# Two engines for the cross products: GpSimd takes three of five chunks in units without gathers

## The chip, the cores and the metric

The kernel runs on one core of a Trainium2 chip. The metric is the device time of one execution, in microseconds (us), lower is better. The core has five engines that run unsynchronised and hand work on by semaphores: TensorE (PE in the profile), VectorE (DVE), ScalarE (ACT), GpSimd (POOL) and SyncE (SP), whose queue issues most of the DMAs.

## The reference

A recommender tower over a batch of 1024 rows, in f32. For each row 50 embeddings of 300 numbers are gathered, two attention heads pool them, and a layer makes h (300 numbers). The heavy part is the product of all pairs of h with a matrix of 44,850 rows:

```python
q1 = _attn_pool(x, mask, w1, b1, w2)
q2 = _attn_pool(x, mask, w3, b3, w4)
h = jnp.concatenate([q1, q2], axis=1) @ w5 + b5
f6 = h @ w6 + b6
iu, ju = jnp.triu_indices(E, k=1)
g = (v @ v.T)[iu, ju]
cross = h[:, iu] * h[:, ju] * g
f7 = cross @ w7 + b7
out8 = jnp.concatenate([f6, f7], axis=1) @ w8 + b8
return jnp.einsum('bu,bku->bk', out8, label_embedding)
```

The last line takes 200 dot products of each row with its own label embeddings (246 MB read once). Three small layers (the top) follow on these 200 results and 16 context numbers.

## The kernel before

The batch is cut into 8 tiles of 128 rows. The cross products of a tile come in 71 units, and two tiles are in work at a time, staggered, so there are 325 units (u = 0 to 324). Units 41 to 283 hold two tiles, units 0 to 40 the first tile alone, and units 284 to 324 the last (tile 7) alone. A unit is a block of five chunks (three in a folded unit). For each unit:

- SP loads `w7` rows of the unit into one of four places of `w_sb` (line 670), which needs the unit four before it used.
- PE turns a block of h into the PSUM tile `coarse` (line 1014), one such window for two units. The other factor lies in SBUF as `fine`, refilled for each part of a round.
- DVE multiplies `fine` by `coarse` into `prod`, all five chunks in one instruction (`cross`, line 930). `prod` has three places, so cross(u) needs unit u-3 used.
- ACT scales each chunk by g (line 1474), in order, and between chunks copies windows, sums absolute values of gathered rows (line 1369) and answers PE's bursts.
- PE multiplies each chunk by its `w7` rows into `acc` (line 1223). The trace has two records for each such product, so a unit of two tiles is 20 records and of one tile 10.

Between the crosses DVE does, in an order fixed by `plan()`, the other work: `dots` (scores of a tile's embeddings, line 772), `wsums` (the weighted sums, line 820, in ten halves a tile), and `slab` (the label dot products, line 772, 8 label rows each; 25 slabs a tile, numbered 0 to 199 through the batch). A slab of a tile needs the tile's out8, which comes after its 71st unit. Nine slabs of tile 7 are multiplied by GpSimd (line 746) and summed by ACT (line 1379). The slabs are loaded by SP too (line 692), in one queue with the `w7` loads, in the order of the table `LOADS`. A slab's load waits for its place to be free: 4 places, later 10, and 3 more for the end.

GpSimd issues the gathers of the embeddings, one instruction a field (line 711), 50 a tile, in groups of five, each group behind the weighted sums of the tile before it that free its rows. When a tile's slabs are all done, its top (four bursts on PE: line 1072, 1078, 1085, 1123) runs where `schedule()` finds room.

`plan()` walks through time with a table of costs (0.1 us each) and writes down which item DVE takes behind which cross, and the order of the loads.

Of the kernel before, what the change touches and what calls it, by code (L numbers as in the profile page):

```python
# [13 lines left out]
P = 128  # L14
# [8 lines left out]
FINE = 5  # L23
# [39 lines left out]
DIAGS = 10  # L63
JUNK = 3
LAB_FIELDS = SLOTS * SLAB
# [140 lines left out]

def plan():

# [23 lines left out]
    while c < TOTAL or len(slab_end) < len(slabs):  # L232
        u, nslab, due, held = c - 1, len(slab_end), 1e9, False
        if c < TOTAL:
            due = FIRST_CROSS if c < 2 else begun[c - 2] + 0.45 * UNIT[len(active(c - 2))]
            held = bool(rest) and c > STARTS[rest[0][1]] - 8
            if now >= due and not held:
                now = max(now, ended[c - RING]) + CROSS[len(active(c))]
                begun[c] = max(ended[c - 1], now + 15)
                ended[c] = begun[c] + UNIT[len(active(c))]  # L240
                if c + W7_RING < TOTAL:
                    loads.append((ended[c], "w7", c + W7_RING))
                c += 1
                continue
# [75 lines left out]


BEFORE, ITEMS, TAIL, POOL_TICKS, LOADS, SWITCH = plan()
LABELLED = {item[1]: u for u in range(TOTAL) for item in ITEMS[u] if item[::2] == ("slab", SLABS - 1)}

# [107 lines left out]
def order_last_loads(loads):  # L432


    extra = [("slab", LAST + END_SLOTS + n) for n in range(EXTRA_SLOTS)]
    loads = [load for load in loads if load not in extra]
    loads.insert(loads.index(("w7", TOTAL - 1)) + 1, extra[0])
    loads.insert(loads.index(("slab", LAST + END_SLOTS - 2)), extra[1])
    loads.insert(loads.index(("slab", LAST + END_SLOTS - 1)) + 1, extra[2])
    return loads  # L440
# [10 lines left out]
def dlrm_tower(nc, ids, tables, labels, ctx_in, w_score, b_rep, w5, w6, b7_in, w7, w8a_in, w8b,  # L451
               v_i, v_j, top1, bias1, top2, bias2, top3, ident_in, y_out):
    with ExitStack() as ctx:
# [18 lines left out]
        top3_sb = sb("top3_sb", [P, M2])  # L472
        pads = sb("pads", [P, FIELDS])
        g_all = sb("g_all", [P, CHUNKS])
# [17 lines left out]
        dup = sb("dup", [P, 2, 2, P])  # L492
        picked = sb("picked", [P, PICKED, 2, P])
        prod = sb("prod", [P, RING, FINE, 2 * P])
        w7_sb = sb("w7_sb", [P, W7_RING, FINE * EMB])
# [3 lines left out]
        big = sb("big", [P, 2 * ECN * P])  # L499
        small = sb("small", [P, EMB])  # L500
        qt = big[:, 0:QCN * P]
# [3 lines left out]
        h1t = big[:, 0:M1 * P]  # L505
        f7s = small[:, 0:EMB]
        zt = small[0:ZC, 0:ZCN * P]
# [63 lines left out]
        fine_ready = sem("fine_ready")  # L571
        chunk_ready = sem("chunk_ready")
        unit_used = sem("unit_used")
        pe_step = sem("pe_step")
# [69 lines left out]
        def _(sp):  # L644
# [20 lines left out]
            for kind, n in LOADS:  # L665
# [14 lines left out]
                elif n == LAST + END_SLOTS:  # L680
                    sp.wait_ge(cross_ready, FREE_FINE)
                elif n == LAST + END_SLOTS + 1:
                    sp.wait_ge(unit_used, PAIR_USED)
# [13 lines left out]
        def _(pool):  # L697
# [51 lines left out]
        def _(dve):  # L749
            dve.memset(ones, 1.0).then_inc(filled, 1)  # L750
            dve.memset(pads[:], PAD).then_inc(filled, 1)
            for r in range(JUNK):
# [36 lines left out]
            def mask(t):  # L789
# [5 lines left out]
                for head in range(2):  # L795
                    dve.copy_predicated(score[:, t % 2, head, :], empty[:], pads[:]).then_inc(chain, 1)
                then(t, 4)
# [190 lines left out]
        def _(pe):  # L988
# [14 lines left out]
            def turn_coarse(u):  # L1003
# [6 lines left out]
                if w >= 2:  # L1010
                    pe.wait_ge(cross_ready, last_unit(w - 2) + 1)
                rows = rows_of(u)
                for t in active(u):
# [225 lines left out]
        def _(act):  # L1239
# [10 lines left out]
            def pick_window(u):  # L1250
# [215 lines left out]
            for u in range(TOTAL):  # L1466
                rows = rows_of(u)
                slot, n = slots_of(u)
                act.wait_ge(cross_ready, u + 1)
                for m in range(FINE):  # L1470
                    if m < chunks_of(u):
                        chunk = prod[0:rows, u % RING, m, slot * P:(slot + n) * P]
                        pair = u % UNITS * FINE + m
# [7 lines left out]
                    for name, t, i in POOL_TICKS.get(tick, ()):  # L1481
# [4 lines left out]
                        elif name == "exp_softmax":  # L1486
                            exp_softmax(t)
            respond("f7s", TILES - 1, 0, 0)
            for name, of, n in END_BURSTS:
                for summed in {"zt": range(2), "z_first": range(2, FIRST_SUMS),  # L1490
                               "z_rest": range(FIRST_SUMS, len(BY_POOL))}.get(name, ()):
                    sum_rows(summed)
                respond(name, of, n, TILES % 3)
# [91 lines left out]
```

## Time and profile before

| | |
|---|---|
| median of 3 runs | 1827.76 us (1826.76 to 1828.46) |
| the profiled execution | 1827.58 us |
| its span, first to last instruction | 1825.8 us |
| PE busy, share of the span | 1686.1 us, 92% |
| DVE busy | 1658.0 us, 91% |
| ACT busy | 1014.6 us, 56% |
| POOL busy | 576.0 us, 32% |
| mean granted clock of TensorE | 0.975 |
| moved by DMA | 561.69 MB, mean 308 GB/s |

Busy time is the time in which an engine had an instruction in work. Matmuls overlap and their ends are modelled. The 1.8 us around the span are not in the trace.

### The profile page before, as it was taken

The numbers are of one execution on the slowest core, as the hardware profiler recorded it, in microseconds if no ns is written. First come the engines' busy times: TensorE is split into PE (matmuls) and PEld (weight loads), VectorE is DVE, ScalarE is ACT, GpSimd is POOL, SyncE is SP. The second block draws the span as 40 slices with busy tenths as digits, with TensorE's granted clock in tenths as the row PEclk, the third lists the DMA queues.
The fourth block names the chain that finished last, engine by engine and source line by source line (L and its number), as shares of the span: only waits on it lengthen the run. The fifth ranks groups of instructions, "written<-read, shape, count | busy, mean of one in ns | idle before, by whom it ended". The sixth has DMA issues, their size and how long they took to land.

```text
span 1825.8 us, 25763 instructions
## 1 busy us (share of the span) xinstructions
PE 1686.1 (92%) x6990; PEld 1243.0 (68%) x6990; DVE 1658.0 (91%) x5831; ACT 1014.6 (56%) x3183; POOL 576.0 (32%) x420
## 2 busy tenths in 40 slices
PE   2888999999999999999999999999999999997755
PEld 1645667777767777777777777767776677775545
DVE  5988989989999889999999999899999888957678
ACT  3776693684357644456554674445754344354536
POOL 7777806828300044500067108700000000000027
PEclk8899999999999999999999999999999999999986
DMA  9488856857987689888878866998648999989996
GB/s 276 108 274 297 308 179 209 326 169 278 381 329 296 244 318 373 328 363 322 299 243 307 318 248 204 352 418 352 229 161 341 420 420 377 417 306 419 418 415 264
DMA packets 98221, 561.69 MB, mean 308 GB/s; under 512 B 16799, under 2 KB 17157, under 8 KB 72477
## 3 DMA queue, kind: packets, MB, share of 16 engines
q1 hardware_dynamic: 77917, 498.35, 70.8%
q0 software_dynamic: 19424, 61.65, 10.7%
q8 instruction: 57, 0.93, 0.2%
q14 instruction: 87, 0.71, 0.1%
q10 hardware_dynamic: 736, 0.05, 0.0%
HBM read 559.98 MB, written 0.00 MB: 307 GB/s over the span
## 4 chain that ended last, share of the span: by engine, by line
PE 44%; DVE 33%; DMA 9%; POOL 6%; issue 6%; ACT 2%; SPq 0%; DVEq 0%; POOLq 0%; ACTq 0%
PE acc L1223 38%; DVE junk L772 12%; DVE qa L820 12%; DVE prod L930 8%; DMA w_sb<-in_w 8%; POOL x L711 4%; POOL lab L711 2%; DMA lab<-in_labels 1%; ACT waste L1369 1%; PE coarse L1014 1%; PE acc L1061 1%; PE acc L1064 1%; PE misc L1026 1%; PE coarse L1118 1%; PE acc L1046 1%
## 5 line engine op out<-in xcount | busy, mean ns | idle before, releaser
L1223 PE MATMUL acc<-w_sb,prod 128*128 128x300 f32 (+2 forms) x5648 | 1510.7, 421 | 62.9 <-DMA w_sb<-in_w 35.0
L1223 PEld LDWEIGHTS acc<-w_sb,prod 128*128 128x128 f32 (+2 forms) x5648 | 1048.2, 191 | 430.4 <-issue 52.7
L1474 ACT ACTIVATE prod<-prod,g_all 128x256 f32<-128x256 f32 (+4 forms) x1615 | 675.0, 470 | 477.1 <-DVE prod L930 472.4
L711 POOL DMA_INDIRECT x<-in_tbl,ids_sb x368 | 488.4, 1327 | 644.5 <-DVE qa L820 534.2
L930 DVE TENSOR_TENSOR prod<-fine,coarse 128x1280 f32<-128x1280 f32 (+3 forms) x320 | 418.6, 1314 | 85.1 <-PE coarse L1014 69.3
L772 DVE SCALAR_TENSOR_TENSOR junk<-lab,heads 128x300 bf16<-128x300 f32 x1192 | 471.1, 459 | 12.6 <-DMA lab<-in_labels 7.7
L772 DVE SCALAR_TENSOR_TENSOR junk<-x,heads 128x300 bf16<-128x300 f32 x1112 | 439.0, 460 | 24.0 <-DMA x<-in_tbl,ids_sb 23.6
L820 DVE SCALAR_TENSOR_TENSOR qa<-x,ex,qa 128x300 f32<-128x300 f32 x612 | 275.4, 520 | 0.1
L746 POOL TENSOR_TENSOR x<-x,out 128x2400 f32<-128x2400 f32 x4 | 21.2, 5288 | 583.3 <-ACT out L1326 583.3
L1369 ACT ACTIVATE waste<-x 128x300 bf16<-128x300 f32 x368 | 161.6, 439 | 26.0 <-DMA x<-in_tbl,ids_sb 25.2
L1294 ACT ACTIVATE fine<-misc 128x512 f32<-128x512 f32 (+3 forms) x67 | 36.3, 542 | 112.3 <-PE misc L1026 83.7
L772 DVE DVE_READ_ACCUMULATOR junk<-lab,heads 128x1 f32 x1192 | 96.1, 81 | 0.0
L772 DVE DVE_READ_ACCUMULATOR junk<-x,heads 128x1 f32 x1112 | 90.0, 81 | 0.0
L1369 ACT ACTIVATION_READ_ACCUMULATOR waste<-x 128x1 f32 x368 | 69.3, 188 | 0.0
L1271 ACT ACTIVATE picked<-hh 128x256 f32<-128x256 f32 (+5 forms) x165 | 61.3, 372 | 0.0
L1014 PE MATMUL coarse<-ident,picked 128*128 128x128 f32 (+2 forms) x288 | 58.9, 274 | 0.0
L1014 PEld LDWEIGHTS coarse<-ident,picked 128*128 128x128 f32 (+2 forms) x288 | 40.7, 141 | 24.4 <-issue 0.4
L1198 PE MATMUL acc<-x,fine 128*128 128x300 f32 x88 | 24.6, 443 | 22.0 <-ACT fine L1417 22.0
L711 POOL DMA_INDIRECT lab<-in_tbl,ids_sb x32 | 35.9, 1123 | 9.8 <-issue 9.8
L1198 PEld LDWEIGHTS acc<-x,fine 128*128 128x128 f32 x88 | 17.6, 203 | 29.1 <-issue 21.5
L1078 PE MATMUL acc<-small,top_sb 108*128 108x128 f32 x112 | 15.5, 297 | 14.1 <-ACT small L1248 14.1
L820 DVE SCALAR_TENSOR_TENSOR qa<-lab,ex,qa 128x300 f32<-128x300 f32 x60 | 27.1, 520 | 0.0
(142 smaller groups left out, 604.2 us busy)
## 6 DMA issues: line engine op xcount, KB each, us to landing
w_sb<-in_w SPq DMA_DIRECT2D x320, 750.0 KB, 6.8
lab<-in_labels SPq DMA_DIRECT2D x144, 1200.0 KB, 8.7
x<-in_labels SPq DMA_DIRECT2D x51, 1200.0 KB, 12.0
x<-in_tbl,ids_sb POOLq DMA_INDIRECT x368, 5.5
fine<-in_labels SPq DMA_DIRECT2D x2, 1200.0 KB, 11.1
prod<-in_labels SPq DMA_DIRECT2D x2, 1200.0 KB, 13.6
w_sb<-in_w SPq DMA_DIRECT2D x5, 450.0 KB, 4.5
w_sb<-in_labels SPq DMA_DIRECT2D x1, 1200.0 KB, 12.4
```

The costliest lines, as they stand in the source:

```text
L711: pool.indirect_dma_start(out=row_of(t, n), out_offset=None, in_=tables[n], in_offset=bass.IndirectOffsetOnAxis(ap=ids_sb[:, t % IDS_RING, ...
L746: pool.tensor_tensor(slab_place(slot), slab_place(slot), row8, ALU.mult).then_inc(multiplied, 1)
L772: dve.scalar_tensor_tensor(unused, in0, 1.0, in1, ALU.mult, ALU.mult, accum_out=out).then_inc(rows_done, 1)
L820: dve.scalar_tensor_tensor(part, row_of(t, n), ex[:, head, n:n + 1], part, ALU.mult, ALU.add).then_inc(wsum_done, 1)
L930: dve.tensor_tensor(prod[0:rows, u % RING, 0:chunks, slot * P:(slot + n) * P], sets[0:rows, made:made + chunks, slot * P:(slot + n) * P], ...
L1014: last = pe.transpose(coarse[0:rows, w % 2, t % 2 * P:(t % 2 + 1) * P], picked[:, w % PICKED, t % 2, 0:rows], ident[:])
L1198: pe.matmul(sums[:, head, 0:EMB], diag[:, k % DIAGS, :], x[:, n, :], start=i < 2, stop=i >= PE0[group] - 2).then_inc(diag_used, 1)
L1223: last = pe.matmul(acc[:, t % 3, 0:EMB], prod[0:rows, u % RING, m, t % 2 * P:(t % 2 + 1) * P], w7_sb[0:rows, u % W7_RING, m * EMB:(m + 1) ...
L1271: act.activation(out, cols, ACT.Copy).then_inc(picked_ready, 1)
L1294: act.activation(sets[0:rows, at + ms[0]:at + ms[-1] + 1, slot * P:(slot + tiles) * P], made[:, :, slot * P:(slot + tiles) * P], ACT.Copy) ...
L1369: act.activation(waste[:, n % 2, :], row_of(t, n), ACT.Abs, accum_out=absum[:, t % 2, n:n + 1]).then_inc(abs_done, 1)
L1474: act.activation(chunk, chunk, ACT.Copy, scale=g_all[0:rows, pair:pair + 1]).then_inc(chunk_ready, 1)
```

## The change

In the units in which GpSimd has no gathers to issue (`SHARED`, 177 of 325), DVE's cross makes only the first two chunks. ACT copies the window from PSUM to a new SBUF tile `kept` (91 copies), and GpSimd makes the other three from it (`share_of`). ACT waits for them ahead of the third chunk. The shared units are 37 to 49, 62 to 72, 92 to 108, 132 to 150, 173 to 186, 207 to 234 and 248 to 324, without the folded ones. 133 have two tiles and 44 have one. GpSimd's shares of such a stretch stand in its queue behind the last gather of one tile and ahead of the first gather of the next.

The planner counts 0.7 us for a cross of two tiles where it counted 1.4, so the order of DVE's items and of the loads changes. To make room, `junk` has two places and not three, `pads` is one column read with step 0, and `f7s` moves from `small` to `dup`.

```diff
-JUNK = 3
+JUNK = 2
+SHARE = 3
+POOL_CROSS = (0, 4, 7)
-def plan():
+def plan(pooled):
...
-                now = max(now, ended[c - RING]) + CROSS[len(active(c))]
+                now = max(now, ended[c - RING]) + (POOL_CROSS if c in pooled else CROSS)[len(active(c))]
...
-BEFORE, ITEMS, TAIL, POOL_TICKS, LOADS, SWITCH = plan()
+GATHERS_END = 4
+def free_of_gathers(items):
+    busy = [[u for u in range(TOTAL) for kind, of, _ in items[u] if (kind, of) == ("wsums", t)]
+            for t in range(1, TILES)]
+    until = [units[0] + 1 for units in busy[1:]] + [TOTAL]
+    return [[u for u in range(units[-1] + GATHERS_END, end) if not folded(u)]
+            for units, end in zip(busy, until)]
+PLAN = plan(())
+for _ in range(2):
+    PLAN = plan(frozenset(u for units in free_of_gathers(PLAN[1]) for u in units))
+BEFORE, ITEMS, TAIL, POOL_TICKS, LOADS, SWITCH = PLAN
+AFTER_GATHERS = free_of_gathers(ITEMS)
+SHARED = frozenset(u for units in AFTER_GATHERS for u in units)
+def own_chunks(u):
+    return chunks_of(u) - SHARE * (u in SHARED)
...
@@ GpSimd @@
+            def share_of(u):
+                slot, n = slots_of(u)
+                cols = slice(slot * P, (slot + n) * P)
+                rows, made = rows_of(u), first_set(u) + (not opens(u)) * FINE
+                pool.wait_ge(window_kept, windows_kept(u))
+                pool.wait_ge(fine_ready, fills_before(u))
+                pool.wait_ge(unit_used, u - RING + 1)
+                window = kept[0:rows, cols]
+                window = bass.AP(tensor=window.tensor, offset=window.offset,
+                                 ap=[list(window.ap[0]), [0, SHARE], [1, n * P]])
+                pool.tensor_tensor(prod[0:rows, u % RING, own_chunks(u):FINE, cols],
+                                   fine_sets[0:rows, made + own_chunks(u):made + FINE, cols],
+                                   window, ALU.mult).then_inc(shared_ready, 1)
             for t in range(2, TILES):
...
                     gather(t, n)
...
+                for u in AFTER_GATHERS[t - 2]:
+                    share_of(u)
+            for u in AFTER_GATHERS[TILES - 2]:
+                share_of(u)
@@ VectorE, cross(u) @@
+                if not opens(u) and keeps_window(u - 1):
+                    dve.wait_ge(window_kept, windows_kept(u))
...
-                rows, chunks = rows_of(u), chunks_of(u)
+                rows, chunks = rows_of(u), own_chunks(u)
@@ ScalarE @@
+            def keep_window(u):
+                w = window_of(u)
+                slot, n = slots_of(u)
+                rows, cols = rows_of(u), slice(slot * P, (slot + n) * P)
+                act.wait_ge(coarse_ready, w + 1)
+                act.activation(kept[0:rows, cols], coarse[0:rows, w % 2, cols], ACT.Copy
+                               ).then_inc(window_kept, 1)
...
                 act.wait_ge(cross_ready, u + 1)
+                if keeps_window(u):
+                    keep_window(u)
                 for m in range(FINE):
                     if m < chunks_of(u):
+                        if m == own_chunks(u):
+                            act.wait_ge(shared_ready, shares_up_to(u))
```

The first place is GpSimd's queue, from the gathers of tile 2 on. Before, gathers follow on gathers:

```order
L711 DMA x<-in_tbl,ids_sb 128x300 x18
L705 DMA ids_sb<-in_ids 128x50
L711 DMA x<-in_tbl,ids_sb 128x300 x26
L705 DMA ids_sb<-in_ids 128x50
L711 DMA x<-in_tbl,ids_sb 128x300 x50
L705 DMA ids_sb<-in_ids 128x50
```

Of the change, from the same place:

```order
L760 DMA ids_sb<-in_ids 128x50
L766 DMA x<-in_tbl,ids_sb 128x300 x24
L795 ISA
L795 TENSOR_TENSOR prod<-fine,kept 126x3x128 x4
L795 TENSOR_TENSOR prod<-fine,kept 128x768 x9
L766 DMA x<-in_tbl,ids_sb 128x300 x26
L760 DMA ids_sb<-in_ids 128x50
L766 DMA x<-in_tbl,ids_sb 128x300 x24
L795 TENSOR_TENSOR prod<-fine,kept 128x768 x11
```

The shares of units 37 to 49 (4 of one tile, 9 of two) stand behind the last gather of tile 2, and the shares of units 62 to 72 (x11) behind all 50 gathers of tile 3, which are the 26 and 24 rows ahead of them. An `ISA` row stands ahead of the first product; before it stood ahead of line 746's.

The second place is the end of SP's queue, in the last units. `w_sb<-in_w` is a unit's `w7`, the others are slabs. Before, from the load of unit 318's `w7` on:

```order
L670 DMA w_sb<-in_w 128x1500 x2
L692 DMA lab<-in_labels 128x2400
L670 DMA w_sb<-in_w 128x1500 x2
L692 DMA lab<-in_labels 128x2400
L670 DMA w_sb<-in_w 128x1500
L692 DMA fine<-in_labels 128x2400
L692 DMA x<-in_labels 128x2400
```

Of the change, from the load of unit 316's `w7` on:

```order
L724 DMA w_sb<-in_w 128x1500 x2
L747 DMA lab<-in_labels 128x2400
L724 DMA w_sb<-in_w 128x1500
L747 DMA lab<-in_labels 128x2400
L724 DMA w_sb<-in_w 128x1500
L747 DMA lab<-in_labels 128x2400
L724 DMA w_sb<-in_w 128x1500
L747 DMA x<-in_labels 128x2400
L724 DMA w_sb<-in_w 128x1500 x4
L747 DMA fine<-in_labels 128x2400
```

From slab 160, which stands behind unit 290's `w7` in both, to unit 324's `w7` there are 22 slab loads before and 25 in the change; to unit 320's `w7`, 20 and 24. Slabs 182 to 184 stand behind the last `w7` before, and ahead of it in the change. Over the whole queue the slab loads ahead of unit 240's `w7` go from 109 to 122.

The tops move as well: tile 5's from units 286 to 288 to units 274 to 276, tile 6's from behind the last unit to units 319 to 321.

## Rows read from the trace of the kernel before

**Rows 1.** Busy time (and count) of PE, PEld, DVE, ACT, POOL; granted clock, DMA share, GB/s.

```profile
190.00:1400.00 1210.00, 1191.34 (x5024) 888.89 (x5023) 1166.50 (x3869) 691.05 (x2061) 382.88 (x277) 1.00 0.78 291
1400.00:1640.00 240.00, 233.73 (x996) 175.69 (x995) 196.19 (x754) 107.71 (x285) 0.00 (x0) 0.99 0.97 390
1640.00:1760.00 120.00, 95.40 (x356) 65.03 (x355) 90.26 (x371) 57.57 (x205) 0.00 (x0) 0.96 1.01 419
```

**Rows 2.** PE's waits from 190 to 1640, then to 235: total, times, longest.

```profile
PE acc L1223 <- ACT prod L1474: 13.4, 24, 1.8
PE acc L1223 <- DMA w_sb<-in_w: 10.7, 6, 3.0
...
PE acc L1223 <- ACT prod L1474: 3.6, 7, 1.4
```

**Rows 3.** The tail: GpSimd's first product, two of DVE's rows.

```profile
1767.47 5.25 POOL L746 TENSOR_TENSOR x<-x,out 128x2400 f32<-128x2400 f32 x1 [583.31 <-ACT out L1326]
...
1772.56 0.46 DVE L772 SCALAR_TENSOR_TENSOR junk<-x,heads 128x300 bf16<-128x300 f32 x1
1772.95 0.46 DVE L772 SCALAR_TENSOR_TENSOR junk<-x,heads 128x300 bf16<-128x300 f32 x1
```

**Rows 4.** Groups by form: cross of two tiles, of one, ACT's chunk, GpSimd's product.

```profile
L930 DVE TENSOR_TENSOR prod<-fine,coarse 128x1280 f32<-128x1280 f32 x210 | 310.4, 1480 | 35.9 <-PE coarse L1014 34.1 <-PE acc L1223 1.6 <-issue 0.2
L930 DVE TENSOR_TENSOR prod<-fine,coarse 128x640 f32<-128x640 f32 x60 | 47.9, 815 | 34.9 <-PE coarse L1014 24.0 <-PE acc L1223 10.9
L1474 ACT ACTIVATE prod<-prod,g_all 128x256 f32<-128x256 f32 x1050 | 468.8, 497 | 357.5 <-DVE prod L930 353.3 <-ACT z L1248 2.9 <-issue 1.0
L746 POOL TENSOR_TENSOR x<-x,out 128x2400 f32<-128x2400 f32 x4 | 21.2, 5288 | 583.3 <-ACT out L1326 583.3
```

**Rows 5.** PE's waits at 1412 and 1423, and the clock around them.

```profile
1412.76 4.99 PE L1223 MATMUL acc<-w_sb,prod 126*128 126x300 f32 x12 [2.16 <-DMA w_sb<-in_w]
1423.23 1.47 PE L1223 MATMUL acc<-w_sb,prod 126*128 126x300 f32 x4 [3.02 <-DMA w_sb<-in_w]
...
1410.00:1430.00 20.00, 14.81 (x51) 10.19 (x50) 17.31 (x71) 5.55 (x15) 0.00 (x0) 0.83 1.01 422
```

**Rows 6.** PE in time from unit 61 on: start, us, records.

```profile
349.96 0.38 PE L1014 MATMUL coarse<-ident,picked 128*128 128x128 f32 x2
350.18 10.49 PE L1223 MATMUL acc<-w_sb,prod 128*128 128x300 f32 x40
```

**Rows 7.** GpSimd's gathers of tile 3, 283 to 376 us: the group, then two single ones.

```profile
L711 POOL DMA_INDIRECT x<-in_tbl,ids_sb x50 | 76.3, 1526 | 69.4 <-DVE qa L820 54.8 <-issue 14.6
...
332.00 4.25 POOL L711 DMA_INDIRECT x<-in_tbl,ids_sb  x1 [0.30 <-issue]
...
374.74 0.95 POOL L711 DMA_INDIRECT x<-in_tbl,ids_sb  x1 [0.30 <-issue]
```

**Rows 8.** Tile 4's last gather, and DVE's cross of unit 92.

```profile
505.77 0.95 POOL L711 DMA_INDIRECT x<-in_tbl,ids_sb  x1 [0.30 <-issue]
...
518.59 1.48 DVE L930 TENSOR_TENSOR prod<-fine,coarse 128x1280 f32<-128x1280 f32 x1
```

**Rows 9.** The last gather of tile 2, and PE in unit 37.

```profile
228.43 0.95 POOL L711 DMA_INDIRECT x<-in_tbl,ids_sb  x1 [0.30 <-issue]
...
230.18 1.18 PE L1223 MATMUL acc<-w_sb,prod 126*128 126x300 f32 x4
```

**Rows 10.** SP issues slab 160; PE starts units 320 and 324.

```profile
1626.08 0.33 SPq L692 DMA_DIRECT2D lab<-in_labels  x1
...
1745.16 3.30 PE L1223 MATMUL acc<-w_sb,prod 126*128 126x300 f32 x12 [1.57 <-DMA w_sb<-in_w]
...
1758.33 2.79 PE L1223 MATMUL acc<-w_sb,prod 126*128 126x300 f32 x10 [1.21 <-DMA w_sb<-in_w]
```

**Rows 11.** A slab's load in the page's DMA issues: KB each, us to landing.

```profile
lab<-in_labels SPq DMA_DIRECT2D x144, 1200.0 KB, 8.7
```

**Rows 12.** A burst of tile 5's top on PE.

```profile
1624.17 1.95 PE L1078 MATMUL acc<-small,top_sb 108*128 108x128 f32 x16
```

More of the change, by code:

```diff
@@ L319, in plan, with shares_up_to, keeps_window, windows_kept @@
     return before, items, tail, pool_ticks, loads, switch
-BEFORE, ITEMS, TAIL, POOL_TICKS, LOADS, SWITCH = plan()
+GATHERS_END = 4
[13 more added lines that the diff above has]
+    return chunks_of(u) - SHARE * (u in SHARED)
+def shares_up_to(u):
+    return sum(v in SHARED for v in range(u + 1))
+def keeps_window(u):
+    return u in SHARED and not (u - 1 in SHARED and window_of(u - 1) == window_of(u))
+def windows_kept(u):
+    return sum(keeps_window(v) for v in range(u + 1))
+def windows_kept_up_to(w):
+    return sum(keeps_window(v) for v in range(TOTAL) if window_of(v) <= w)
 LABELLED = {item[1]: u for u in range(TOTAL) for item in ITEMS[u] if item[::2] == ("slab", SLABS - 1)}
@@ L437, in order_last_loads @@
     loads.insert(loads.index(("w7", TOTAL - 1)) + 1, extra[0])
-    loads.insert(loads.index(("slab", LAST + END_SLOTS - 2)), extra[1])
-    loads.insert(loads.index(("slab", LAST + END_SLOTS - 1)) + 1, extra[2])
+    weights_end = loads.index(extra[0]) + 1
+    loads.insert(max(weights_end, loads.index(("slab", LAST + END_SLOTS - 2))), extra[1])
+    loads.insert(max(weights_end + 1, loads.index(("slab", LAST + END_SLOTS - 1)) + 1), extra[2])
     return loads
@@ L472, in dlrm_tower @@
         top3_sb = sb("top3_sb", [P, M2])
-        pads = sb("pads", [P, FIELDS])
+        pad = sb("pad", [P, 1])
+        pads = bass.AP(tensor=pad[:].tensor, offset=pad[:].offset,
+                       ap=[list(pad[:].ap[0]), [0, FIELDS]])
         g_all = sb("g_all", [P, CHUNKS])
@@ L493, in dlrm_tower @@
         picked = sb("picked", [P, PICKED, 2, P])
+        kept = sb("kept", [P, 2 * P])
         prod = sb("prod", [P, RING, FINE, 2 * P])
@@ L499, in dlrm_tower @@
         big = sb("big", [P, 2 * ECN * P])
-        small = sb("small", [P, EMB])
+        small = sb("small", [P, 2 * P])
         qt = big[:, 0:QCN * P]
@@ L505, in dlrm_tower @@
         h1t = big[:, 0:M1 * P]
-        f7s = small[:, 0:EMB]
+        f7s = dup[:].rearrange("p m t b -> p (m t b)")[:, 0:EMB]
         zt = small[0:ZC, 0:ZCN * P]
@@ L572, in dlrm_tower @@
         chunk_ready = sem("chunk_ready")
+        window_kept = sem("window_kept")
+        shared_ready = sem("shared_ready")
         unit_used = sem("unit_used")
@@ L681, in _ @@
                     sp.wait_ge(cross_ready, FREE_FINE)
+                    sp.wait_ge(shared_ready, shares_up_to(FREE_FINE - 1))
                 elif n == LAST + END_SLOTS + 1:
@@ L750, in _ @@
             dve.memset(ones, 1.0).then_inc(filled, 1)
-            dve.memset(pads[:], PAD).then_inc(filled, 1)
+            dve.memset(pad[:], PAD).then_inc(filled, 1)
             for r in range(JUNK):
@@ L795, in mask @@
                 for head in range(2):
-                    dve.copy_predicated(score[:, t % 2, head, :], empty[:], pads[:]).then_inc(chain, 1)
+                    dve.copy_predicated(score[:, t % 2, head, :], empty[:], pads).then_inc(chain, 1)
                 then(t, 4)
@@ L1011, in turn_coarse @@
                     pe.wait_ge(cross_ready, last_unit(w - 2) + 1)
+                    if windows_kept_up_to(w - 2):
+                        pe.wait_ge(window_kept, windows_kept_up_to(w - 2))
                 rows = rows_of(u)
@@ L1488, in _ @@
             respond("f7s", TILES - 1, 0, 0)
+            summed = 0
             for name, of, n in END_BURSTS:
-                for summed in {"zt": range(2), "z_first": range(2, FIRST_SUMS),
-                               "z_rest": range(FIRST_SUMS, len(BY_POOL))}.get(name, ()):
-                    sum_rows(summed)
+                for slab in range(summed, {"zt": 2, "z_first": FIRST_SUMS,
+                                           "z_rest": len(BY_POOL)}.get(name, summed)):
+                    sum_rows(slab)
+                    summed = slab + 1
                 respond(name, of, n, TILES % 3)
```

## The prediction

> **What bounds the kernel now.** I read the busy time in stretches first, then PE's waits, then the timelines at the places where the new queue order matters. From 190 to 1400 us both PE (1191 of 1210) and DVE (1167) look full, the clock is 1.00 and DMA is at 0.78 [rows 1]. PE's idle time is the one that can be won back: 19 us there, 6 us from 1400 to 1640, and by releaser 13.4 us for ACT's chunks and 10.7 us for `w7` [rows 2]. So in the two-tile units PE sets the pace and DVE only just keeps up; what DVE gains shows up to about 24 us and no further. From 1640 to 1760 it is another kernel: one tile, PE busy 95 of 120, DMA share 1.01 at 419 GB/s. Each unit waits for its `w7` behind the slabs in the same queue. After the last unit comes a tail in which GpSimd's nine products run end to end [rows 3] with DVE's rows beside them.
>
> **The change, part by part.**
>
> *DVE.* A cross of 1280 elements takes 1480 ns, one of 640 takes 815 [rows 4]: 1.04 ns an element and 0.15 us fixed. Two chunks of two tiles (512) make 0.68, of one (256) 0.42. Saved: 133 x 0.80 + 44 x 0.40 = 124 us of DVE's time. It is worth only what it takes off PE's waits. Of the 13.4 us for chunks, 3.6 lie before 235 us and unit 37 [rows 2], where nothing is shared. Of the 10.7 us for `w7`, 5.2 are the waits at 1412 and 1423 us [rows 5]. They come from the burst of loads when six more places open: up to unit 251's `w7` that burst has eleven slabs in both tables, so they stay. That leaves 9.8 + 5.5 = 15 us. The lateness stems mostly from units with weighted sums, which are not shared, so I take half: **-7 us** (bounds 0 and -15).
>
> *GpSimd's product.* 2400 elements take 5288 ns [rows 4], 2.2 ns each: 768 make 1.69 us, 384 make 0.85, if time goes with length; above, it is bounded by the row itself, 5.29. ACT's cycle for a unit becomes: copy of the window, about 0.45 (as long as a chunk, 0.50), the product, two handoffs of 0.1, and three chunks of at most 0.50: 3.8 us against PE's 5.16 (20 records in 10.49 us by 40, [rows 6]). It stays hidden up to a product of about 3.0 us. I take 1.69, since the nine products of the tail run at 2.2 ns with DVE's rows beside them. DVE's rows there are 0.39 apart for 300 elements [rows 3], so they aren't slowed either.
>
> What DVE does beside GpSimd matters: a gather takes 4.25 us beside the weighted sums, which have both inputs in SBUF, and 0.95 beside the label rows and scores, whose second input is in PSUM [rows 7]. A cross is of the second kind. Only the shares of a stretch's last unit (49, 72, 108, 150, 186, 234) meet weighted sums and may come 4.25 - 0.95 = 3.3 us late. PE is two units (10 us) behind at that point, so it is hidden; I count **+1** (bounds 0 and 6 x 3.3 = 20, the latter without any cover).
>
> The Trainium skill (SBUF — State Buffer, "Who interferes with whom") has this as a rule: a DVE instruction with two SBUF inputs shuts out a GpSimd instruction that reads SBUF for its whole length, one with a single SBUF input doesn't. The trace agrees for the gathers; by the rule too the sum would be 1863, and against shares laid beside all of DVE's work it would speak loudly.
>
> *The shares of units 62 to 72.* This is the largest term. They stand behind all 50 gathers of tile 3, and the change moves none of those: their pace is set by the weighted sums in units 49 to 58, which aren't shared. GpSimd gathers until 374.74 + 0.95 = 375.7 [rows 7]; after the last `qa` beside it, near 336, it issues one each 1.25 us (0.95 and 0.30 of issue) and waits for nobody, so it is simply behind. PE starts unit 62 at 350.18 + 16 records x 0.26 = 354.3 and its third chunk at 356.4 [rows 6]. In the change that chunk is there at 375.7 + 1.69 + 0.2 + ACT's 0.50 = 378.1. ACT waits ahead of it, DVE at cross 65 (its place in `prod` is not free), SP with its `w7` loads: nothing covers it. **+21.7 us.** The idle PE then loses clock: after waits of 2 and 3 us the clock was 0.83 over 20 us [rows 5], 3.4 us; over the 10 us behind one wait **+1.7**. Fifty gathers take 92 us here; the later stretches have their weighted sums over 17 or more units, not ten. There GpSimd keeps up: tile 4's gathers end 12 us ahead of cross 92, where the next stretch of shares begins [rows 8].
>
> *Unit 37.* The last gather of tile 2 ends at 229.4, PE takes the third chunk at 230.2 [rows 9]. With 0.3 + 0.85 + 0.1 + 0.39 it comes at 231.0, and ACT, full with sums of absolute values there, is some 2 us behind afterwards: **+3** (bounds 1 and 7: the first product as long as the row of 2400 elements, 5.3 us for 0.85, adds 4). The Trainium skill (GPSIMD Engine Reference, "Instruction dispatch") gives about 6 us for the first call of a freshly loaded GpSimd routine; if the ISA row is such a load, the term would be 9 and the sum 1869 by it. No row here shows it: before, it fell in idle time.
>
> *The last stage.* Slab 160's load is issued at 1626.08, after tile 6's out8, in both orders; unit 320 starts at 1745.16 when its `w7` lands [rows 10]. A slab is 1200 KB [rows 11], at 419 GB/s 2.93 us. The change puts four more slabs ahead of unit 320's `w7`: +11.7. From there before needed 15.9 us to the end of unit 324 (1761.1); now the four `w7` come in a row and PE is the limit: 5 x 2.58 plus tile 6's top, 4.3 us (1.8 for a burst like that of [rows 12], 1.95 less its overlap, twice, and 0.7 for two small ones) makes 17.2: +1.3. Tile 5's top, 4.3 us, was in the time after slab 160's issue, where PE had to wait for data anyway; now it is in units that PE bounds: +4.3. Against it, PE without that top reaches the DMA's limit sooner after slab 160, so a little of the 119 us comes back; I take -2. Together **+15** (bounds 5 and 18). Nothing is given back in the tail: it has three loads fewer, but its length is nine products of 5.22 us on GpSimd and ACT's sums behind them, started by out8.
>
> *Two places for junk.* A row waits for the one two before it. That ended 0.32 us before this one starts (0.39 apart, 0.46 long [rows 3]), and its accumulator is read at once: nothing. The rest (`pads`, `dup`) moves no work.
>
> **Sum.** 1827.6 (the profiled execution, 0.2 below the median) - 7 + 1 + 21.7 + 1.7 + 3 + 15 = **1863 us**, 1.9% slower.
>
> **The rivals.**
> 1. *The last stage is neutral* (0.14). If the slabs' order there is free, because DVE or the places hold SP up before the bandwidth does, the 15 us fall away: 1848. For it: SP waits for slab places all through. Against: share 1.01 for 120 us.
> 2. *GpSimd is free by unit 62* (0.05). If the five gathers of a group took 7 us, as the planner counts, and not 9.2, the 23.4 us fall away: 1840. Against: the last gather's row [rows 7].
> 3. *DVE paces it* (0.04), the one that ends faster. 97 two-tile units between 41 and 247 save 0.80 each, 77 us. If PE's records hid waits for DVE, these would come out: 1828 - 77 + 42 = 1793. It decides once DVE costs PE more than 42 us there; the trace shows 13.4 [rows 2].
> 4. *GpSimd's product is longer than 3.0 us* (0.06), by a fixed cost or by standing still beside DVE. At 4 us ACT's cycle is about 6.1: 0.9 x 133 on top, about 1980.
> 5. *Rivals 1 and 2 together* (0.03) make 1825, within 0.2% of before.
>
> That the change doesn't free DVE, because DVE waits for `kept` as long as it saves, only takes the 7 us away: 1870, within the forecast's own range.
>
> The forecast itself has 0.68, its own range 1850 to 1878. 0.2% (3.7 us) is what a measurement can tell. Faster 0.04, same 0.03, slower 0.93. The range of 1842 to 1886 takes in rival 1 and the bounds of unit 37, of the shares beside weighted sums and of the 15 us; it leaves out rivals 2 to 5.
>
> **What the profile after would show.** GpSimd goes from its last gather of tile 3 straight to eleven products; PE has one wait of about 20 us for ACT's chunk near 360 us, and DVE one just as long a little later, with a dip of the clock. GpSimd's product of 128x768 takes 1.7 us. PE's `w7` waits at 1410 to 1430 (shifted by some 25 us) are still there; between slab 160's issue and unit 320 lie about 129 us and not 119. The tail from out8 is as long as before. If the wait near 360 us is short, or the last stage isn't longer, the forecast falls with it; a PE wait for ACT in most shared units would be rival 4.

## The result, and the profile after

The changed kernel takes 1875.0 us (median of 4, 1871.3 to 1878.5) against 1827.6 for the kernel before beside it: a ratio of 1.026 [1.024, 1.028]. The forecast was 1863 with a range of 1842 to 1886. Slower was right, and the wait forecast at unit 62 was right to a tenth. The shares earn more than the forecast had, the new table costs more, and a part of the table's cost had no term at all. The profiled execution took 1878.5 us, 50.9 more than before's.

The busy time in stretches answers to [rows 1]; the columns are the same, and the stretches are moved by the time lost ahead of them:

```profile
190.00:1400.00 1210.00, 1165.54 (x4903) 869.14 (x4902) 1107.91 (x3984) 693.40 (x2079) 537.99 (x379) 0.99 0.79 296
1400.00:1680.00 280.00, 266.03 (x1122) 197.53 (x1121) 158.00 (x661) 130.36 (x347) 75.15 (x47) 0.99 0.80 315
1680.00:1811.00 131.00, 102.30 (x384) 68.27 (x383) 72.85 (x347) 61.20 (x219) 29.01 (x30) 0.93 0.99 406
```

DVE was busy 1166 us in the first stretch and is now busy 1108: it has been freed, as planned. PE, which set the pace, is busy 26 us less in the same time, so it stands more. The second line holds what the forecast did not have: the DMA share from 1400 on was 0.97 and is 0.80.

PE's waits from 190 to 1690 answer to [rows 2]:

```profile
PE acc L1302 <- ACT prod L1566: 42.2, 28, 21.6
PE acc L1302 <- DMA w_sb<-in_w: 18.4, 14, 3.1
```

One wait makes half of the first line. The timeline of GpSimd and then of PE, and the clock over 20 us, at units 62 and 63 ([rows 6, 7] are the same place before):

```profile
378.17 0.95 POOL L766 DMA_INDIRECT x<-in_tbl,ids_sb  x1 [0.30 <-issue]
379.15 1.81 POOL L795 TENSOR_TENSOR prod<-fine,kept 128x768 f32<-128x768 f32 x1
...
381.55 6.90 PE L1302 MATMUL acc<-w_sb,prod 128*128 128x300 f32 x16 [21.65 <-ACT prod L1566]
...
373.00:393.00 20.00, 11.45 (x36) 8.34 (x37) 9.04 (x43) 11.65 (x41) 10.13 (x8) 0.65 0.28 85
```

The first product begins directly behind the last gather, and PE's third chunk of unit 62 comes 21.65 us late. The granted clock averaged 0.65 over the 20 us around the end of that wait. Taken in parts it was 0.50 from 381 to 385 us, so PE began again at 1.2 GHz and not at 2.4, and 0.89 in the 8 us behind. The DMA share is down to 0.28 over the 20 us: the places of `w_sb` come free only as PE goes on.

Unit 37, to be set beside [rows 9]:

```profile
229.67 1.96 POOL L795 TENSOR_TENSOR prod<-fine,kept 126x384 f32<-126x384 f32 x2
...
231.17 1.50 PE L1302 MATMUL acc<-w_sb,prod 126*128 126x300 f32 x4 [2.93 <-ACT prod L1566]
```

The groups by form of DVE's two chunks, GpSimd's product for two tiles and for one, ACT's copy of the window, and GpSimd's product of the tail, beside [rows 4]:

```profile
L1007 DVE TENSOR_TENSOR prod<-fine,coarse 128x512 f32<-128x512 f32 x110 | 75.3, 684 | 153.9 <-ACT kept L1361 69.9 <-PE coarse L1093 47.8 <-issue 29.9
L795 POOL TENSOR_TENSOR prod<-fine,kept 128x768 f32<-128x768 f32 x110 | 197.9, 1820 | 424.4 <-ACT kept L1361 418.7 <-PE acc L1302 5.7
L795 POOL TENSOR_TENSOR prod<-fine,kept 128x384 f32<-128x384 f32 x30 | 29.6, 998 | 91.7 <-ACT kept L1361 82.1 <-PE acc L1302 9.4
L1361 ACT ACTIVATE kept<-coarse 128x256 f32<-128x256 f32 x57 | 21.4, 375 | 46.3 <-DVE prod L1007 46.1
L821 POOL TENSOR_TENSOR x<-x,out 128x2400 f32<-128x2400 f32 x4 | 21.0, 5258 | 10.6 <-ACT out L1414 10.6
```

DVE's price, taken from the slope of [rows 4], held: 0.684 us and 0.68 forecast. GpSimd's, taken in proportion to the length, was 1.69 and is 1.82: 768 and 384 elements show a fixed 0.18 us under the 2.1 ns an element. GpSimd is idle ahead of its two-tile products for 418.7 us, waiting for the copy, so it has time to spare once its gathers are done. But two engines now wait that didn't before, ACT for GpSimd's product and DVE for the copy:

```profile
ACT prod L1566 <- POOL prod L795: 75.8, 66, 22.4
DVE prod L1007 <- ACT kept L1361: 117.5, 18, 10.7
```

Of ACT's 75.8 us, 22.4 are unit 62. DVE's 117.5 us are nearly as much as the 124 us that the shares save it. The forecast named this case, in which the change doesn't free DVE. What these waits cost by themselves was not tested; the shares paid with such waits in place (58.6 us of them in the kernel `share_clean` below).

In the last stage SP issues slab 160, PE begins its last 30 records (units 322 to 324), and GpSimd's tail begins ([rows 10] and [rows 3] before):

```profile
1664.07 0.33 SPq L747 DMA_DIRECT2D lab<-in_labels  x1
...
1803.37 7.84 PE L1302 MATMUL acc<-w_sb,prod 126*128 126x300 f32 x30
...
1817.55 10.46 POOL L821 TENSOR_TENSOR x<-x,out 128x2400 f32<-128x2400 f32 x2 [10.61 <-ACT out L1414]
```

PE ends unit 324 at 1811.2, 147.1 us after slab 160's issue, where before needed 135.0. From GpSimd's first product of the tail to the end of the span it is 59.0 us, before 58.3: the tail gave nothing back.

### The profile page after: what moved, and what is told of

Same layout as the page of the kernel before. It is cut to its first block, busy times and chain, and to the rows that moved or that the text cites. A ratio compares the mean times of both kernels' runs of the same rounds, so it can differ in the third digit from the quotient of the medians.

```text
span 1876.6 us, 26315 instructions
## 1 busy us (share of the span) xinstructions
PE 1692.3 (90%) x6990; PEld 1244.2 (66%) x6990; DVE 1545.9 (82%) x5830; ACT 1043.3 (56%) x3274; POOL 834.7 (44%) x597
## 4 chain that ended last, share of the span: by engine, by line
PE 41%; DVE 31%; DMA 10%; POOL 9%; issue 6%; ACT 2%; SPq 0%; ACTq 0%; DVEq 0%; POOLq 0%
PE acc L1302 35%; DVE junk L847 16%; DVE qa L895 8%; DMA w_sb<-in_w 8%; POOL x L766 7%; DVE prod L1007 6%; POOL lab L766 2%; DMA lab<-in_labels 2%; PE misc L1105 1%; PE coarse L1093 1%; ACT waste L1457 1%; PE acc L1125 1%; PE coarse L1197 1%; ACT prod L1566 1%; PE acc L1140 1%
## 5 line engine op out<-in xcount | busy, mean ns | idle before, releaser
L1566 ACT ACTIVATE prod<-prod,g_all 128x256 f32<-128x256 f32 (+4 forms) x1615 | 682.5, 470 | 428.7 <-DVE prod L1007 347.4
L795 POOL TENSOR_TENSOR prod<-fine,kept 128x768 f32<-128x768 f32 (+3 forms) x177 | 283.8, 1622 | 739.1 <-ACT kept L1361 722.1
L766 POOL DMA_INDIRECT x<-in_tbl,ids_sb x368 | 463.8, 1260 | 269.3 <-DVE qa L895 160.5
L1007 DVE TENSOR_TENSOR prod<-fine,coarse 128x512 f32<-128x512 f32 (+7 forms) x320 | 296.2, 930 | 257.4 <-ACT kept L1361 117.5
L847 DVE SCALAR_TENSOR_TENSOR junk<-lab,heads 128x300 bf16<-128x300 f32 x1256 | 496.7, 462 | 6.4 <-DMA lab<-in_labels 3.7
L847 DVE SCALAR_TENSOR_TENSOR junk<-x,heads 128x300 bf16<-128x300 f32 x1048 | 413.3, 462 | 23.4 <-DMA x<-in_tbl,ids_sb 22.9
L847 DVE DVE_READ_ACCUMULATOR junk<-lab,heads 128x1 f32 x1256 | 104.7, 83 | 0.0
L1361 ACT ACTIVATE kept<-coarse 128x256 f32<-128x256 f32 (+3 forms) x91 | 31.8, 349 | 74.0 <-DVE prod L1007 73.8
L1277 PEld LDWEIGHTS acc<-x,fine 128*128 128x128 f32 x88 | 17.8, 206 | 28.4 <-issue 21.1
```

The source lines that it names most:

```text
L766: pool.indirect_dma_start(out=row_of(t, n), out_offset=None, in_=tables[n], in_offset=bass.IndirectOffsetOnAxis(ap=ids_sb[:, t % IDS_RING, ...
L795: pool.tensor_tensor(prod[0:rows, u % RING, own_chunks(u):FINE, cols], fine_sets[0:rows, made + own_chunks(u):made + FINE, cols], window, ...
L847: dve.scalar_tensor_tensor(unused, in0, 1.0, in1, ALU.mult, ALU.mult, accum_out=out).then_inc(rows_done, 1)
L1007: dve.tensor_tensor(prod[0:rows, u % RING, 0:chunks, slot * P:(slot + n) * P], sets[0:rows, made:made + chunks, slot * P:(slot + n) * P], ...
L1277: pe.matmul(sums[:, head, 0:EMB], diag[:, k % DIAGS, :], x[:, n, :], start=i < 2, stop=i >= PE0[group] - 2).then_inc(diag_used, 1)
L1566: act.activation(chunk, chunk, ACT.Copy, scale=g_all[0:rows, pair:pair + 1]).then_inc(chunk_ready, 1)
```

## The experiments

Two parts of the change can be separated. `AFTER_GATHERS` (and `SHARED`, made from it) says which units are shared. The planner's lower price for shared units (`POOL_CROSS`) says where the items between units stand, and with them the label slabs and the order of the loads. I call the table that the planner gives at the old price the old table.

**Where the shares wait for gathers.** `late62` begins the second stretch of shares at unit 67:

```diff
 AFTER_GATHERS = free_of_gathers(ITEMS)
+AFTER_GATHERS[1] = [u for u in AFTER_GATHERS[1] if u >= 67]
```

> The changed kernel, with units 62 to 66 taken out of the shared ones (VectorE makes all five of their chunks), so that the stretch behind tile 3's gathers begins at unit 67; order of items and loads unchanged. Theory T (shares of unit 62 stand behind the last gather, PE waits 21.65 us there and loses a few more to the clock): no such wait, about 25 us less, 1850 us (1845 to 1856). Rival R1 (the shares cost their time everywhere, by the wait for the kept copy and GpSimd's own pace, and unit 62 only shows what would come elsewhere): 1870 us or more. Rival R2 (the delay at unit 62 is given back later, since VectorE then has room): 1872 to 1878 us.

1855.6 us (1853.6 to 1858.3), 19.4 below the changed kernel. The long wait is gone, and R1 and R2 fall. It is 19.4 and not 25 in part because a wait of 3.31 us at unit 65, which the long one had covered, now shows (below). `late62_37` leaves out units 37 to 40 as well:

```diff
+AFTER_GATHERS[0] = [u for u in AFTER_GATHERS[0] if u >= 41]
+AFTER_GATHERS[1] = [u for u in AFTER_GATHERS[1] if u >= 67]
```

> As late62, and units 37 to 40 not shared either (that stretch begins at unit 41). Theory T: the 2.93 + 0.43 us of PE's waits at unit 37 and the clock behind them go as well, 3 to 6 us less than late62: about 1845 us (1840 to 1851). Rival (the 3 us at unit 37 are the first product's own start-up and move to unit 41): equal to late62 within 1 us.

1854.0 us (1852.7 to 1854.3). Less than expected: 1.6 us, and the two kernels' times overlap, so a cost of unit 37 isn't shown clear of the noise. PE has no wait above 0.5 us from unit 37 to 45, so nothing moved there either. But 26.4 us over before are left, with no unit waiting for a gather. (R1 to R9 are the rivals in these expectations; those of the prediction are called by their numbers below.)

**Shares without the new table, and the table without shares.** `share_old_order` takes away the planner's second and third pass:

```diff
 PLAN = plan(())
-for _ in range(2):
-    PLAN = plan(frozenset(u for units in free_of_gathers(PLAN[1]) for u in units))
```

> The shares of the changed kernel with the planner's table of the kernel before: items between the units and order of the loads are those of before (182 slabs ahead of the last w7 block, not 185), 194 units are shared. Theory T: units 62 and 37 still wait (25 + 6 us), the last stage and the label batches fall back to before's (the 15 to 20 us of the later part go): 1858 us (1852 to 1865). Rival R1 (the sharing itself costs in the last stages, by GpSimd's pace or contention): 1873 us or more. Rival R3 (VectorE's freed time pays once the order is old): 1850 us or less.

1865.1 us (1858.6 to 1868.2), a tenth above T's range. With this table two more stretches begin ahead of their tile's last gather. PE's waits at units 37, 62, 177 and 207:

```profile
230.44 3.81 PE L1300 MATMUL acc<-w_sb,prod 126*128 126x300 f32 x7 [2.95 <-ACT prod L1564]
...
380.66 3.87 PE L1300 MATMUL acc<-w_sb,prod 128*128 128x300 f32 x7 [21.71 <-ACT prod L1564]
...
1030.68 2.37 PE L1300 MATMUL acc<-w_sb,prod 126*128 126x300 f32 x4 [9.06 <-ACT prod L1564]
...
1215.21 2.37 PE L1300 MATMUL acc<-w_sb,prod 128*128 128x300 f32 x4 [14.50 <-ACT prod L1564]
```

They make 48.2 us, more than the whole 37.5 that this kernel is over before. So something pays. `order_alone` is the other half, the new table with DVE doing all five chunks:

```diff
-AFTER_GATHERS = free_of_gathers(ITEMS)
+AFTER_GATHERS = [[] for _ in range(1, TILES)]
```

> The changed kernel's order of items and loads, but no unit is shared: VectorE makes all five chunks everywhere, as before. Theory T: no waits at units 62 and 37; the order costs 15 to 20 us in the last stages as in the changed kernel, and some more where items stand between units for which VectorE has no time now: 1852 us (1843 to 1870). Rival R1 (the sharing costs, the order is free): 1828 to 1833 us.

1890.8 us (1890.0 to 1891.8): 63 over before, far beyond both theories' numbers. The direction was T's, the size was not. PE's waits from 190 to 1690 account for 39 of the 63 (62.7 us, where [rows 2] has 24.1 up to 1640); ACT's chunks are late 50 times and not 24:

```profile
PE acc L1302 <- ACT prod L1566: 50.1, 50, 3.3
PE acc L1302 <- DMA w_sb<-in_w: 12.6, 9, 3.2
```

The table has work placed for a DVE that is quicker in the shared units, and without shares DVE has not the time. It means too that on this table the shares are worth 15.8 us even with their wait at unit 62, and 36.8 without it (`late62_37`).

**The shares alone.** `share_clean` is `share_old_order` with each stretch beginning where the last gather is over:

```diff
 AFTER_GATHERS = free_of_gathers(ITEMS)
+AFTER_GATHERS = [[u for u in units if u >= first]
+                 for units, first in zip(AFTER_GATHERS, (41, 70, 92, 140, 182, 212, 248))]
```

> The shares of the changed kernel with the planner's table of before (as share_old_order), and each shared stretch begins only where the tile's last gather is over in that run's trace (units 41, 70, 92, 140, 182, 212 and 248 on): 168 units are shared. Theory T (what costs is units that stand behind gathers, and the new order; the sharing itself neither costs nor pays, since PE's own work and, at the end, the loads of w7 set the pace): 1829 us (1824 to 1835). Rival R1 (GpSimd's pace, the kept copy or contention cost in every shared unit): 1840 us or more. Rival R3 (VectorE's freed time pays once nothing waits for gathers): 1820 us or less.

1815.5 us (1813.6 to 1816.8), a ratio to before of 0.993 [0.991, 0.995]: a small gain, but clear of the noise, and 59.5 us under the changed kernel. My theory (1829) missed by 13 us; R3 came out. The four waits for gathers, 48.2 us, account for nearly all of the 49.6 us between `share_old_order` and this kernel. `old_order_alone` is the control, with the changed kernel's other edits, the old table and no share:

```diff
+AFTER_GATHERS = [[] for _ in range(1, TILES)]
```

> The changed kernel's code with the planner's table of before and no shared unit: only its other edits are left (two junk buffers, the constant of one column, the f7s copy in the dup buffer, the smaller scratch, the end's bookkeeping). Theory T (the 12 us that share_clean gained on before come from the sharing, by fewer of PE's waits for chunks in units 90 to 250): 1827.5 us within 2. Rival R6 (they come from the other edits): about 1815 us.

1827.9 us, ratio 1.0007 [0.9997, 1.0016]. The gain is the shares'. `clean_to248` drops the last stretch of shares, 76 units:

```diff
-                 for units, first in zip(AFTER_GATHERS, (41, 70, 92, 140, 182, 212, 248))]
+                 for units, first in zip(AFTER_GATHERS, (41, 70, 92, 140, 182, 212, TOTAL))]
```

> share_clean without its last stretch: units 248 to 324 are not shared, 92 units are. Theory T (from unit 248 on PE's own work and then the loads set the pace, and the gain was made before): as share_clean, 1815.5 us (1812 to 1819). Rival R7 (VectorE's freed time in the last stages carries part of the gain, through earlier slabs): 1820 to 1828 us.

1814.9 us (1813.5 to 1816.2), as `share_clean`. Ninety-two shared units do all of it; from 248 on the shares earn nothing.

**What the new table costs, in two places.** `price284` is `late62_37` with the lower price only up to unit 283:

```diff
-    PLAN = plan(frozenset(u for units in free_of_gathers(PLAN[1]) for u in units))
+    PLAN = plan(frozenset(u for units in free_of_gathers(PLAN[1]) for u in units if u < 284))
```

> late62_37 with the planner's lower price for shared units only up to unit 283; from unit 284 on the units are shared all the same, but planned at the old price. 183 slabs stand ahead of the last w7 block, not 185, and tile 6's top goes back behind the last unit. Theory T (the last one-tile stage is bound by its loads, each slab ahead of the last w7 costs its 2.9 us, and tile 6's top delays the units behind it): 2 x 2.9 + 4 to 8 us less than late62_37's 1854: 1843 us (1837 to 1848). Rival R4 (work taken out of the last stage comes back in the tail, one for one): 1851 to 1856 us.

1844.8 us (1843.5 to 1845.7), 9.2 below `late62_37`, and nothing came back in the tail (65.5 us from PE's last chunk, 65.7 there). Four slabs fewer stand ahead of unit 320's `w7` (180 and not 184), and two fewer ahead of the last. `top6_late` moves the other thing that stood in the last stage, tile 6's top:

```diff
-        if tick + 16 > TOTAL * FINE:
+        if tick + 16 > TOTAL * FINE or t == TILES - 2:
```

> late62_37 with tile 6's top put behind the last unit, as before, and nothing else moved (slabs as in the changed kernel, 185 ahead of the last w7 block). Theory T: PE's end of the last unit comes 4 to 8 us earlier and the tail takes the top beside VectorE's rows: 1848 us (1844 to 1851). Rival R4: it lay in PE's waits for w7 anyway, or the tail pays it back: 1853 to 1856 us.

1853.6 us (1850.9 to 1856.5), as `late62_37`. R4 was right here and T wrong: the top's four bursts, 5.1 us of PE's work in the changed kernel's profile (0.63, 1.95, 1.95 and 0.60), lie in time in which PE would have waited for `w7`. So the stage is bound by what is loaded, and the slabs make the 9 to 11 us by which `price284` is shorter. The last pair splits the table at unit 200. `price_to200`, on the changed kernel:

```diff
-    PLAN = plan(frozenset(u for units in free_of_gathers(PLAN[1]) for u in units))
+    PLAN = plan(frozenset(u for units in free_of_gathers(PLAN[1]) for u in units if u < 200))
...
 AFTER_GATHERS = free_of_gathers(ITEMS)
+AFTER_GATHERS = [[u for u in units if u >= first]
+                 for units, first in zip(AFTER_GATHERS, (41, 70, 92, 132, 173, 207, 248))]
```

> Shares as in late62_37 (168 units less three: the second stretch begins at 70), planned at the lower price only up to unit 199; from 200 on at the old price. 180 slabs stand ahead of the w7 block of unit 320, as before, 183 ahead of the last. Theory T (the new order costs in two separate places, some 13 us before unit 200 against share_clean's table, and the rest in tile 5's burst of slabs and the last stage): 1815.5 + 13 + 4 to 10 for the burst at units 260 to 276 and the slab more: 1835 us (1829 to 1842). Rival R8 (the early part of the order costs nothing that is not given back): 1820 us or less.

1830.5 us (1827.9 to 1836.3): 15.0 over `share_clean`. R8 falls. And `price_from200`:

```diff
-    PLAN = plan(frozenset(u for units in free_of_gathers(PLAN[1]) for u in units))
+    PLAN = plan(frozenset(u for units in free_of_gathers(PLAN[1]) for u in units if u >= 200))
...
 AFTER_GATHERS = free_of_gathers(ITEMS)
+AFTER_GATHERS = [[u for u in units if u >= first]
+                 for units, first in zip(AFTER_GATHERS, (41, 70, 92, 140, 182, 212, 248))]
```

> share_clean with the lower price planned only from unit 200 on; the table up to unit 199 is that of before. 184 slabs stand ahead of the w7 block of unit 320 (180 before), 185 ahead of the last, and tile 5's slabs come in units 258 to 277. Theory T: share_clean plus 8 us for tile 5's burst plus 9 to 13 for the slabs ahead of the last w7 blocks: 1835 us (1830 to 1840), PE waiting for w7 there. Rival R9 (the late costs hang on the early order, which moved the switch to ten slots): 1822 us or less.

1836.2 us (1835.9 to 1836.7): 20.7 over `share_clean`. R9 falls. The two halves make 35.7 of the 38.5 us between `share_clean` and `late62_37` (whose stretches begin a few units earlier, at 67, 132, 173 and 207).

**Junk.** `junk2` is the kernel before with one line changed:

```diff
-JUNK = 3
+JUNK = 2
```

> The kernel before with JUNK = 2 and nothing else: the running rows of the slab products turn over two buffers, not three. Theory T (nobody reads them, the engine writes in order): 1827.6 us within 1.5. Rival R5 (a product waits for the one two before): about 0.06 us for each of 3,000 rows that wait, 1835 us or more.

1828.0 us, ratio 1.0002 [0.9992, 1.0011]. The term of nothing was right.

## Why the prediction came out as it did

By medians the way from before to the changed kernel is: the shares alone -12.0, the new table +38.5, unit 37 +1.6, unit 62 +19.4, together +47.5. The forecast had -7 + 1, +15, +3 and +23.4, together +35.4. The table's term is the one that failed: it was 23.5 us too small, and the other three, each too high, took 11.4 of that back. That the sum lies only 12 us off is in part luck. The parts hold for this order of steps alone; without shares the same table costs 62.9 us (`order_alone` against `old_order_alone`).

Each kernel's profile gives the time from DVE's cross of one unit to that of another; the last column ends with PE's last chunk of unit 324.

| us from unit to unit | 62-90 | 130-200 | 200-286 | 286-end |
|---|---|---|---|---|
| before | 152.9 | 394.1 | 485.4 | 148.9 |
| old_order_alone | 153.0 | 395.0 | 485.5 | 149.3 |
| share_clean | 153.8 | 389.7 | 479.5 | 149.1 |
| price_to200 | 159.6 | 398.6 | 478.9 | 152.1 |
| price_from200 | 153.8 | 389.3 | 487.5 | 162.8 |
| late62_37 | 159.7 | 398.6 | 492.0 | 160.5 |
| price284 | 159.5 | 398.6 | 491.8 | 149.8 |
| changed kernel | 178.7 | 398.6 | 491.9 | 160.2 |

*The shares of units 62 to 72* (+21.7 and +1.7). Right by the mechanism and the size of the wait: 21.65 us. DVE stood from 364.5 to 383.95 ahead of the cross of unit 64, one unit sooner than I had it and for another reason: not for a place in `prod`, but for ACT's copy of the window, which stands in ACT's queue behind the chunks of unit 62 and ends 0.08 us before that cross begins.

```profile
383.51 0.36 ACT L1361 ACTIVATE kept<-coarse 128x256 f32<-128x256 f32 x1
...
383.95 0.69 DVE L1007 TENSOR_TENSOR prod<-fine,coarse 128x512 f32<-128x512 f32 x1 [19.45 <-issue]
```

The clock took more than the forecast: the 16 records behind the wait needed 6.90 us, 16 x 0.26 = 4.2 at full clock. With the old table the same wait makes 23.8 us (units 62 to 90 take 177.6 us in `share_old_order` and 153.8 in `share_clean`), as forecast. With the new one the kernel without it is only 19.4 faster, because there is another wait three units later, which the long one covered.

*GpSimd's product, DVE's share, the cycle of ACT.* Right. 1.82 us is well under the 3.0 at which ACT's cycle would have shown, PE doesn't wait for ACT in most shared units, and rival 4 fell.

*Shares beside weighted sums* (+1). The rule of [rows 7] holds for products as well. Of 133 products of 768 elements 132 took 1.81 to 1.84 us, whatever label rows, scores or crosses DVE had beside them. The exception is the one that met the rows of the weighted sums with two SBUF inputs (`x` and `qa`), in the last unit of a stretch:

```profile
637.56 2.73 DVE L895 SCALAR_TENSOR_TENSOR qa<-x,ex,qa 128x300 f32<-128x300 f32 x6
...
638.94 3.03 POOL L795 TENSOR_TENSOR prod<-fine,kept 126x768 f32<-126x768 f32 x1 [10.49 <-ACT kept L1361]
```

It came 1.2 us late, not 3.3, and PE did not wait. The Trainium skill (SBUF — State Buffer, "Who interferes with whom") has this rule: a DVE instruction with two SBUF inputs contends with a GpSimd instruction that reads SBUF. The trace agrees, 3.03 us against 1.81.

*Unit 37* (+3). PE waited 2.93 + 0.43 us there, but the kernel gains only 1.6 when the units are left out. The 6 us for loading a routine that the Trainium skill names (GPSIMD Engine Reference, "Instruction dispatch") do not show: the first product began 0.09 us after the last gather's end and took the normal time, 1.96 us for two.

*Relief of PE* (-7, bounds 0 and -15). The shares alone are worth 12.0. It is found where DVE had only just kept up: 1.9 us less in units 90 to 130, 4.4 in units 130 to 200, 5.9 in units 200 to 286. PE's idle time between the crosses of units 36 and 286 is 22.1 us before and 17.8 in `share_clean`, and its busy time 1370.5 and 1364.3 for 5772 records in both. So 4.2 us are waits, and 6.1 are chunks that take less time one with the other. Up to 3.8 of these can be the clock, which dips less often: 0.97 before and 1.00 in `share_clean` from 500 to 560 us, 0.91 and 0.96 from 1400 to 1440. What shortens the rest is not settled. `old_order_alone`, without shares, lies between the two with 1368.8.

*The last stage* (+15). For the slabs this was right: unit 286 to the end takes 149 us with the old table's loads and 160 to 163 with the new table's last stage, with shares or without (`order_alone` 161.1). Three slabs more stand ahead of the last `w7`, 185 and not 182, at 2.93 us each 8.8; four more ahead of unit 320's, 11.7. But I had put 1.3 us for tile 6's top on it, and that is free. In `price_from200` the late half of the table costs 20.7 by medians; its profile has 13.7 more in the last stage and 8.0 more in units 200 to 286. With the whole table (`late62_37`) that column is 12.5 longer. There the loads of the slabs come in bursts: SP issues none from 1412 to 1468 us, slabs 135 to 159 from then to 1555 us, and none again until 1639. The last ten of them are tile 6's, which can't be used before that tile's products end with unit 283, so all ten places are full. Stretches that begin near units 246, 268 and 281, for `share_clean` and then for `late62_37`:

```profile
1376.00:1506.00 130.00, 123.68 (x532) 93.32 (x531) 98.04 (x445) 60.09 (x152) 36.06 (x20) 0.99 1.01 418
1506.00:1576.00 70.00, 70.00 (x286) 52.70 (x285) 52.13 (x237) 29.68 (x72) 21.86 (x12) 1.00 1.00 393
1576.00:1636.00 60.00, 58.60 (x265) 43.93 (x263) 33.40 (x153) 35.17 (x112) 18.96 (x16) 1.00 0.87 332
```

```profile
1400.00:1530.00 130.00, 125.37 (x536) 93.85 (x535) 80.32 (x365) 59.20 (x149) 39.54 (x22) 0.99 0.86 344
1530.00:1600.00 70.00, 63.00 (x272) 46.56 (x271) 29.62 (x126) 28.95 (x74) 17.98 (x10) 1.00 0.82 329
1600.00:1660.00 60.00, 55.81 (x233) 41.06 (x232) 27.76 (x123) 33.50 (x105) 18.97 (x16) 1.00 0.67 245
```

In the 70 us of the second line PE idles 7.0 us, all of it waits for `w7`, where it was never idle with the old table; in the next 60 the DMA share is 0.67. The forecast named only the burst at 1412 us and had no term for a second one. But the first burst costs less in return: over the whole column PE waits 11.6 us for `w7` in `late62_37` and 8.5 in `share_clean`, so the bursts explain 3 of the 12.5 us. Tile 5's top, which lies in this column too, is 38 records and about 5 us (4.3 in the forecast).

In `price_from200` the 8.0 us are another thing. Its `w7` waits in the column are 10.8 us, 2.3 more, and lie ahead of unit 266, the largest at 1184, 1405 and 1415 us (3.33, 2.45 and 3.35). Behind them the clock was lower: the granted clock over the column is 0.98, where `share_clean` has 1.00. The two together are enough for the 8.0, though no run parts them.

*The early half of the table* had no term at all. The forecast treated the items between units 41 and 247 as moved free of charge, because DVE was the quicker there. `price_to200` has it at 15.0; against `share_clean` its profile has 14.7 us more in the columns 62-90 and 130-200 and 3.0 more in the last (one slab more), less 2 elsewhere. The planner counts a shared unit's cross as half as long and puts two half scores (ten rows each) behind the cross of unit 64. DVE's crosses of units 64 and 65 and PE's wait behind them (unit 65), in `late62_37`:

```profile
360.77 1.48 DVE L1009 TENSOR_TENSOR prod<-fine,coarse 128x1280 f32<-128x1280 f32 x1
369.92 1.48 DVE L1009 TENSOR_TENSOR prod<-fine,coarse 128x1280 f32<-128x1280 f32 x1
...
372.08 1.30 PE L1304 MATMUL acc<-w_sb,prod 128*128 128x300 f32 x4 [3.31 <-ACT prod L1568]
```

9.15 us lie between two crosses where PE needs one each 5.2. A share saves DVE 0.8 us, a half score takes 3.9. Part of this one wait can come from the experiment itself: units 62 to 66 are planned as shared here, but DVE makes all five of their chunks (1.48 us and not 0.68). Three more waits of the kind, of 1.86, 1.42 and 1.43 us at 936, 970 and 992 us, follow units 163, 169 and 173, behind which a slab stands together with a half of the weighted sums or scores. In the two columns PE waits 11.6 us for chunks in `price_to200` and 2.2 in `share_clean`: 9.4 of the 14.7. Of the other 5, 1.8 can be the clock behind the wait of 3.31 us (0.91 from 370 to 390 us, where `share_clean` has 1.00); the rest is in no wait that the profile shows.

Rival 1 (a neutral last stage) is out by `price284`, rival 2 by the gather's row, rival 3 in its size (12 us to win, not 77), though its sign is right once the two costs are taken off. Rival 5 falls with 1 and 2.

## What to carry to other kernels

Giving an idle engine work in a queue costs what stands ahead of it in that queue: four stretches that began behind unfinished gathers cost 49.6 us (`share_old_order`) where the shares themselves earned 12. Change an assignment and the schedule's prices in separate steps; here the planner, told that units had become cheaper, moved work by whole items of 3 to 4 us to use savings of 0.8, and drew the slabs forward in the queue of loads. The new table turned 12 us won into 26 lost. In a stage bound by loads, read the number of transfers ahead of the last one that compute needs, not what the engines have to do.

## What the runs showed of the hardware beyond that

- GpSimd's product of 768 elements took 1.82 us and of 384 took 1.00, in all but one of 177 products: 2.1 ns an element and 0.18 us fixed.
- Behind a wait of 21.65 us PE's granted clock was 0.50 for 4 us and 0.89 over the next 8, and 16 records took 6.90 us.
- Some 5 us of PE's work (tile 6's top) taken out of a stage with a DMA share of 0.99 changed little there: the stage took 160.5 us with it and 159.4 without, and the medians of the two kernels are 0.4 us apart.
- Of the 6.1 us by which an equal count of PE's records is shorter in `share_clean`, at least 2.3 stay open.
